# Laying out softmax denominators by DMA instead of TensorE in a fused attention and FFN block

## The chip, the cores and the metric

One core of one Trainium2 chip runs the kernel. The metric is the device time of one execution in microseconds (us); lower is better. A core has five engines with instruction streams of their own (TensorE or PE, VectorE or DVE, ScalarE or ACT, GpSimd or POOL, SyncE or SP) and DMA engines that the SP queue feeds here.

## The reference

Four batches of 1024 tokens with 128 features go through a layer norm, then grouped-query attention (16 heads of width 64, K and V projected to 512 columns and repeated twice) and a small FFN of hidden size 384; both results are added to the input. All is float32.

```python
xq = rope(q @ Wq); xk = jnp.repeat(rope(kv @ Wk), 2, axis=-1)
xv = jnp.repeat(kv @ Wv, 2, axis=-1)
scores = softmax(xq @ xk * scale, axis=-1)
out = (scores @ xv) @ Wo
h = silu(x @ wg.T) * (x @ wu.T);  ffn = h @ wd.T
x = x + attention(layernorm(x)) + ffn(layernorm(x))
```

The repeat makes neighbouring columns of K and V equal, so the kernel works with 32 distinct features per head (`E` = 32).

## The kernel before

A prologue (about the first 107 us) does the layer norm, the whole FFN and the first projections. After it come 16 steps (4 batches by 4 groups `g` of 4 heads) of two units each; unit `u` = 2s + t is one half of the queries (512 columns, `HALF`) of step `s`. Each of the 32 units has one slot of the main loop. All five streams are written out by hand; they meet only by semaphores, each engine takes its instructions in order, and all DMAs of the loop go through SP's queue.

In slot `u` TensorE (lines 532 to 651) makes, interleaved over eight key tiles `kt`: the scores of unit `u` (line 542, ACT turns each into `prob`, line 799); 16 score tiles of unit `u+1` for its row maxima (`max_tile`, line 379, two places in PSUM; DVE reduces each, line 853, and PE needs the place of tile m-2 free before tile m); the product with V (line 394); the denominators of unit `u-1` (lines 404 and 407); the output projection of unit `u-2` (line 430); and the projections for unit `u+4` (lines 361 and 369).

The part that is changed brings the output of unit `u-1` to `o_norm`. The denominators stand in `bank_m` as 128 x 512: each of four heads has its 512 numbers repeated on 32 partitions. ACT copies them to `den` (`read_den`, line 766, at kt 2). PE transposes `den` in four blocks at kt 3 (`transpose_den`, line 414), so that a head's 512 numbers lie on 128 partitions; DVE inverts the 128 x 16 that are distinct (line 950, after maxima tile 9); ACT spreads them (line 771, at kt 4); PE transposes back (`transpose_inv`, line 421, at kt 5); and DVE multiplies (`normalise`, line 956). `normalise` stands in DVE's order after the 16th tile and `split_max` (lines 859 and 861), and ahead of `pair_sum` (line 946) and `rotate` (lines 844 to 848). `rotate` frees the PSUM places of the projections; the first two maxima tiles of the next slot wait for its two `rope_done` signals (line 560).

SP's order in step `s` (lines 293 to 333), of which the first part falls into slot 2s: an x load (four steps have one: 0, 2, 6 and 10), 12 packs of the lower half (`pack_heads(1 - n, 0)`, 128 KB each), weights, tables (2 MB), V, `wo_stage`, 12 packs of the upper half, V, and the maxima of unit 2s+1 (`pack_max`). The second part falls into slot 2s+1: once a batch the store of the output and a reload of `y_acc`, then the maxima of unit 2s+2. Slot 2s+1 starts on PE only once all 26 packs of step `s` have landed (line 576).

## Time and profile before

| | us |
|---|---|
| runs (3): median, lowest, highest | 1169.87, 1164.29, 1173.73 |
| the profiled execution | 1166.32 |
| its span, first to last instruction | 1164.4 |
| busy: PE, DVE, POOL, ACT | 1118.8, 886.7, 877.2, 733.7 |
| mean granted clock of TensorE | 0.989 |
| one slot of the main loop | 32.6 |

A line of the lists below has the source line, the engine, the operation, what is written and read, how often, the busy time and the mean in ns of one, and the idle time of the engine ahead of it with what ended it. A timeline's line starts with the start time and the duration in us. SPq is the queue of SyncE; its lines show how long it took to issue DMAs, not the transfers. Times in the text without a slot named are those of slot 14 (step 7), which runs from about 567 to 599.5 us, or of slot 15 behind it.

### The profile page before, as it was taken

What the parts mean: (1) busy time and instruction counts of PE and PEld (TensorE: products, weight loads), DVE (VectorE), ACT (ScalarE), POOL (GpSimd) and SP (SyncE); (2) the same over time, 40 slices, a digit from 0 to 9 for tenths busy, and PEclk for the clock granted to TensorE, in tenths of its full rate; (3) what the DMA queues carried; (4) which work ended last, traced back from release to release, by engine and by line L of the source; (5) the groups of instructions that cost most, each with busy time, mean ns of one, the idle gap of its engine ahead of it and who ended that gap; (6) DMA issues with size and microseconds to landing.
All of it is one profiled execution on the core that took longest, in us unless ns stands there. A gap on an engine that the chain in (4) does not pass through costs nothing.

```text
span 1164.4 us, 17083 instructions
## 1 busy us (share of the span) xinstructions
PE 1118.8 (96%) x6288; PEld 661.8 (57%) x6288; DVE 886.7 (76%) x1009; ACT 733.7 (63%) x1330; POOL 877.2 (75%) x274
## 2 busy tenths in 40 slices
PE   5899999999999999999999999999999999999986
PEld 4787555555555565555555555555556555554432
DVE  7686777778787887778787887778788787777721
ACT  3333666666676666766666666666666666666663
POOL 3222778887778888877778887878778887888776
PEclk9899999999999999999999999999999999999999
DMA  6662808071441618071441618071431617050000
GB/s 230 167 258 87 238 2 224 1 222 40 111 115 35 191 37 224 2 222 40 115 110 39 187 37 224 1 218 44 122 105 45 181 37 225 1 130 2 4 1 18
DMA packets 56305, 124.97 MB, mean 107 GB/s; under 512 B 7968, under 2 KB 19488, under 8 KB 54048
## 3 DMA queue, kind: packets, MB, share of 16 engines
q1 hardware_dynamic: 56224, 123.89, 36.8%
q8 instruction: 50, 0.82, 0.3%
q14 instruction: 31, 0.25, 0.1%
HBM read 53.08 MB, written 10.49 MB: 55 GB/s over the span
## 4 chain that ended last, share of the span: by engine, by line
PE 80%; DVE 15%; ACT 2%; issue 1%; POOL 1%; DMA 1%; POOLq 0%; ACTq 0%; DVEq 0%
PE bank_o L394 20%; PE bank_s L542 19%; PE scores L379 18%; DVE row_max L853 13%; PE scores L361 7%; PE bank_m L369 3%; PE bank_m L430 2%; PE bank_m L407 2%; PE bank_m L404 2%; ACT prob L799 2%; PE scores L480 2%; PE bank_s L497 1%; POOL prob_sum L1048 1%; PE bank_o L497 1%; PE bank_m L497 1%
## 5 line engine op out<-in xcount | busy, mean ns | idle before, releaser
L799 ACT ACTIVATE prob<-bank_s 128x512 f32<-128x512 f32 x1024 | 595.5, 600 | 253.4 <-PE bank_s L542 230.0
L853 DVE TENSOR_REDUCE row_max<-scores 128x1 f32<-128x1024 f32 x512 | 597.0, 1214 | 201.3 <-PE scores L379 201.1
L1048 POOL TENSOR_TENSOR prob_sum<-prob_sum,prob 128x2048 f32<-128x2048 f32 x96 | 439.3, 4576 | 13.9 <-ACT prob L799 0.5
L542 PE MATMUL bank_s<-qk_pack 98*128 98x512 f32 x1024 | 431.0, 437 | 8.2 <-ACT prob L799 5.9
L379 PE MATMUL scores<-qk_pack 96*128 96x512 f32 x1024 | 337.4, 411 | 9.0 <-DVE row_max L853 1.4
L542 PEld LDWEIGHTS bank_s<-qk_pack 98*128 98x128 f32 x1024 | 192.9, 189 | 195.1 <-issue 86.9
L394 PE MATMUL bank_o<-prob,v 128*32 128x512 f32 x2048 | 250.0, 606 | 0.0
L1048 POOL TENSOR_TENSOR prob_sum<-prob_sum,prob_pair 128x2048 f32<-128x2048 f32 x32 | 147.2, 4601 | 104.3 <-DVE prob_pair L946 104.3
L379 PEld LDWEIGHTS scores<-qk_pack 96*128 96x128 f32 x1024 | 180.1, 190 | 73.8 <-DVE row_max L853 52.3
L992 POOL TENSOR_TENSOR qk_stage<-rope,qk_stage 128x512 fp32r<-128x512 f32 x64 | 82.0, 1283 | 91.1 <-ACT qk_stage L685 91.1
L1040 POOL TENSOR_TENSOR prob_sum<-prob 128x2048 f32<-128x2048 f32 x32 | 146.8, 4587 | 0.0
L394 PEld LDWEIGHTS bank_o<-prob,v 128*32 128x32 f32 x2048 | 53.8, 110 | 121.5 <-issue 72.7
L361 PE MATMUL scores<-x_stage,w_stage 128*128 128x512 f32 x336 | 98.7, 402 | 0.0
L766 ACT COPY den<-bank_m 128x512 f32<-128x512 f32 x32 | 18.8, 587 | 91.8 <-PE bank_m L407 91.8
L946 DVE TENSOR_TENSOR prob_pair<-prob 128x2048 f32<-128x2048 f32 x32 | 73.8, 2306 | 1.4 <-ACT prob L799 1.4
L361 PEld LDWEIGHTS scores<-x_stage,w_stage 128*128 128x128 f32 x336 | 61.5, 190 | 14.8
L369 PEld LDWEIGHTS bank_m<-w_stage,x_stage 128*128 128x128 f32 x336 | 46.3, 191 | 3.6
L1056 POOL TENSOR_TENSOR y_acc<-y_part,y_acc 128x512 f32<-128x512 f32 x32 | 40.9, 1279 | 8.9 <-ACT y_part L777 8.9
L844 DVE TENSOR_TENSOR scores<-scores,table 128x512 f32<-128x512 f32 x64 | 44.2, 691 | 2.5 <-PE scores L361 2.5
L848 DVE TENSOR_TENSOR rope<-scores,rope 128x512 f32<-128x512 f32 x64 | 44.3, 692 | 2.2
L369 PE MATMUL bank_m<-w_stage,x_stage 128*128 128x128 f32 x336 | 43.8, 266 | 0.0
L846 DVE TENSOR_TENSOR rope<-scores,table 128x512 f32<-128x512 f32 x64 | 43.5, 679 | 0.1
(88 smaller groups left out, 685.0 us busy)
## 6 DMA issues: line engine op xcount, KB each, us to landing
qk_pack<-qk_stage SPq DMA_DIRECT2D x384, 128.0 KB, 4.7
table<-tables SPq DMA_DIRECT2D x16, 2048.0 KB, 9.7
w_stage<-w_scratch SPq DMA_DIRECT2D x14, 640.0 KB, 4.5
v<-v_stage SPq DMA_DIRECT2D x32, 256.0 KB, 7.9
xT_scratch<-xT_hl SPq DMA_DIRECT2D x4, 1024.0 KB, 10.1
x_stage<-xT_scratch SPq DMA_DIRECT2D x4, 1024.0 KB, 6.5
w_scratch<-w_split SPq DMA_DIRECT2D x1, 2560.0 KB, 15.5
x_all<-x SPq DMA_DIRECT2D x4, 512.0 KB, 11.7
```

The costliest lines, as they stand in the source:

```text
L361: last = mm(scores[:, c, :], w_from[:, a, c, :], x_from[:, r, cols], start=n == 0, stop=n == 2)
L369: last = mm(bank_m[:, j * 128:(j + 1) * 128], x_from[:, r, at:at + 128], w_from[:, a, 4, :], start=n == 0, stop=n == 2)
L379: last = mm(scores[:, 2 * (m % places) + c, :], qk_pack[n][0:SPLIT_K, 0, t, h, (m % QT) * 128:(m % QT + 1) * 128], qk_pack[n][0:SPLIT_K, 1 ...
L394: last = mm(bank_o[h * E:(h + 1) * E, :], v_sb[n][:, kt, h * E:(h + 1) * E], prob[:, kt % RING, h, :], start=kt == 0, stop=kt == KT - 1)
L542: mm(bank_s[:, h % 2, :], qk_pack[j][0:SCORE_K, 1, kt // QT, h, (kt % QT) * 128:(kt % QT + 1) * 128], qk_pack[j][0:SCORE_K, 0, t, h, :], s ...
L799: A(prob[:, kt % RING, h, :], bank_s[:, h % 2, :], ACT.Exp).then_inc(prob_ready, 1)
L848: V.tensor_tensor(rope[:, 2 * k, :], scores[:, 2 * k, :], rope[:, 2 * k + 1, :], ALU.add).then_inc(rope_done, 1)
L853: V.tensor_reduce(row_max[:, m:m + 1], scores[:, at:at + 2, :].rearrange("p c k -> p (c k)"), axis=AX.X, op=ALU.max).then_inc(max_read, 1)
L946: V.tensor_tensor(prob_pair[:], prob[:, 4 % RING], prob[:, 5 % RING], ALU.add).then_inc(pair_done, 1)
L992: TT(qk_stage[:, 2 * k + 1, t, :], rope[:, 2 * k, :], qk_stage[:, 2 * k, t, :].bitcast(F32), ALU.subtract).then_inc(lo_done, 1)
L1040: TT(prob_sum[:, t], prob[:, 0], prob[:, 1], ALU.add).then_inc(sum_done, 1)
L1048: TT(prob_sum[:, t], prob_sum[:, t], part, ALU.add).then_inc(sum_done, 1)
```

## The change

- The denominators: SP issues `lay_den`, a DMA that takes one partition of each head from `den` (4 x 512) and lays it out as 64 x 32 in `den_rows`. DVE inverts these 64 x 32 (after maxima tile 11, before it was 9), `save_inv` stores them in DRAM (8 KB), and `spread_inv` reads them back into `den`, each head's row on 32 partitions (256 KB written). Each of the three waits for the one before. `normalise` then reads `den` in place of `bank_m`.
- Both groups of four transposes on PE, the spreading copy on ACT and the small inverse from PSUM are gone from each unit.
- In an even slot the three DMAs of unit 2s-1 are put among the upper packs: `lay_den` before them, `save_inv` after six of the twelve, `spread_inv` after nine. In an odd slot those of unit 2s come after `pack_max` (and after the store and reload, where there is one) and before the next `pack_max`.
- `load_tables` and its wait move ahead of the lower packs.
- PE's transpose of the maxima waits for `den_read` instead of `o_done`; `read_den` waits for the `o_done` of the unit before.
- The last unit has no DMA: DVE inverts all 128 x 512 of `bank_m` into `den`.

```diff
--- before.py
+++ after.py
@@ -69,7 +69,7 @@
 NE = HG
-INVERT_AFTER = 9
+INVERT_AFTER = 11
 def build(nc, x, tables, w_qkv, wo_even, wo_odd, w_gu, w_down, ident_in, out):
@@ -81,6 +81,7 @@
     xT_dram = nc.dram_tensor("xT_scratch", (128, 2, B * S), F32, kind="Internal").ap()
     w_dram = nc.dram_tensor("w_scratch", (128, G, 2, NW), F32, kind="Internal").ap()
     y_dram = nc.dram_tensor("y_scratch", (128, NT, D), F32, kind="Internal").ap()
+    inv_dram = nc.dram_tensor("inv_scratch", (HG, HALF), F32, kind="Internal").ap()
     ctx = ExitStack()
     with ctx:
@@ -107,7 +108,8 @@
         max_rows = keep("max_rows", [2 * TILES, 128])
         o_raw = keep("o_raw", [128, HALF])
         den = keep("den", [128, HALF])
-        den_inv = keep("den_inv", [128, QT, HG])
+        den_rows = keep("den_rows", [2 * E, HALF // QT // 4])
+        inv_rows = keep("inv_rows", [2 * E, HALF // QT // 4])
         y_part = keep("y_part", [128, HALF])
         o_norm = keep("o_norm", [128, HALF])
         y_acc = keep("y_acc", [128, KT, D])
@@ -176,8 +178,8 @@
         score_ready, prob_ready, pv_done, pair_done, sum_done, den_ready = (sem("score_ready"),
             sem("prob_ready"), sem("pv_done"), sem("pair_done"), sem("sum_done"), sem("den_ready"))
-        o_read, den_read, denT_ready, inv_done, inv_spread, inv_ready = (sem("o_read"), sem("den_read"),
-            sem("denT_ready"), sem("inv_done"), sem("inv_spread"), sem("inv_ready"))
+        o_read, den_read, den_laid, inv_done, inv_saved, inv_spread = (sem("o_read"), sem("den_read"),
+            sem("den_laid"), sem("inv_done"), sem("inv_saved"), sem("inv_spread"))
         o_done, y_ready, y_read, y_added = sem("o_done"), sem("y_ready"), sem("y_read"), sem("y_added")
         block = ctx.enter_context(nc.Block())
@@ -233,8 +235,8 @@
                     sp.dma_start(qk_pack[n][r * E:(r + 1) * E, :, t, h, :].bitcast(F32),
                                  qk_stage[h * E:(h + 1) * E, parts, t, :].bitcast(F32)).then_inc(done, 16)
-            def pack_heads(n, t):
-                for h in range(HG):
+            def pack_heads(n, t, heads=range(HG)):
+                for h in heads:
                     pack_head(n, t, h, packed)
             def pack_v(n, t):
@@ -287,6 +289,21 @@
             for n in range(4):
                 sp.wait_ge(y_saved[n], 16 * len(range(n, CHUNKS, 4)) - (16 if n < 2 else 0))
+            def lay_den(u):
+
+                sp.wait_ge(den_read, u + 1)
+                sp.dma_start(den_rows[:], den[0:128:E, :]).then_inc(den_laid, 16)
+
+            def save_inv(u):
+
+                sp.wait_ge(inv_done, u + 1)
+                sp.dma_start(inv_dram.rearrange("h (r c) -> (h r) c", c=HALF // QT // 4), inv_rows[:]).then_inc(inv_saved, 16)
+
+            def spread_inv(u):
+
+                sp.wait_ge(inv_saved, 16 * u + 16)
+                sp.dma_start(den[:], inv_dram.unsqueeze(1).to_broadcast([HG, E, HALF])).then_inc(inv_spread, 16)
+
             def store_out(b):
                 sp.dma_start(out[bass.ds(b, 1)].rearrange("b (n p) d -> p (b n) d", p=128), y_acc[:]).then_inc(out_done, 16)
@@ -299,6 +316,8 @@
                     sp.wait_ge(proj_ready, 10 * s + 20)
                     if new_x:
                         load_x(b + 1 if nxt % G == 0 else b)
+                    sp.wait_ge(rope_done, 4 * s + 8)
+                    load_tables(nxt % G)
                 if not (last_pair and n == 1):
                     at_least(sp, score_ready, 64 * s)
@@ -308,17 +327,25 @@
                     if new_x:
                         sp.wait_ge(xb_in, 16 * (b + (2 if nxt % G == 0 else 1)))
                     load_w(nxt % G)
-
-                    sp.wait_ge(rope_done, 4 * s + 8)
-                    load_tables(nxt % G)
                 if not (last_pair and n == 1):
                     sp.wait_ge(v_staged, 2 * s + 3)
                     at_least(sp, pv_done, 16 * s)
                     pack_v(1 - n, 0)
                 sp.dma_start(wo_stage[n][:], wo_sum[:, g, :]).then_inc(wo_in, 16)
-                if not (last_pair and n == 1):
+                more = not (last_pair and n == 1)
+                if s > 0:
+                    lay_den(2 * s - 1)
+                if more:
                     sp.wait_ge(lo_done, 4 * s + 8)
-                    pack_heads(1 - n, 1)
+                    pack_heads(1 - n, 1, range(2))
+                if s > 0:
+                    save_inv(2 * s - 1)
+                if more:
+                    pack_heads(1 - n, 1, range(2, 3))
+                if s > 0:
+                    spread_inv(2 * s - 1)
+                if more:
+                    pack_heads(1 - n, 1, range(3, HG))
                     sp.wait_ge(v_staged, 2 * s + 4)
                     pack_v(1 - n, 1)
                 pack_max(2 * s + 1, n, 1)
@@ -329,6 +356,9 @@
                     store_out(b - 1)
                     sp.wait_ge(out_done, 16 * b)
                     sp.dma_start(y_acc[:], y_dram[:, bass.ds(b * KT, KT), :]).then_inc(y_in, 16)
+                lay_den(2 * s)
+                save_inv(2 * s)
+                spread_inv(2 * s)
                 if not (last_pair and n == 1):
                     pack_max(2 * s + 2, 1 - n, 0)
@@ -406,20 +436,6 @@
                 for h in range(HG):
                     last = mm(bank_m[h * E:(h + 1) * E, :], ones[:], prob_sum[:, t, h, :], start=False, stop=True)
                 last.then_inc(den_ready, 1)
-
-            def transpose_den(u):
-
-                pe.wait_ge(den_read, u + 1)
-                for j in range(QT):
-                    last = nc.tensor.transpose(bank_m[:, j * 128:(j + 1) * 128], den[:, j * 128:(j + 1) * 128], ident[:])
-                last.then_inc(denT_ready, 1)
-
-            def transpose_inv(u):
-
-                pe.wait_ge(inv_spread, u + 1)
-                for j in range(QT):
-                    last = nc.tensor.transpose(bank_m[:, j * 128:(j + 1) * 128], den[:, j * 128:(j + 1) * 128], ident[:])
-                last.then_inc(inv_ready, 1)
             def project_out(u, n, s):
@@ -604,8 +620,6 @@
                         score(kt, 3)
                         maxima()
                     elif kt == 3:
-                        if not is_first(u):
-                            transpose_den(u - 1)
                         score(kt, 1)
                         maxima()
                         score(kt, 2)
@@ -620,8 +634,6 @@
                         score(kt, 3)
                         maxima()
                     elif kt == 5:
-                        if not is_first(u):
-                            transpose_inv(u - 1)
                         score(kt, 1)
                         maxima()
                         score(kt, 2)
@@ -634,7 +646,7 @@
                         score(kt, 2)
                         if do_max:
-                            at_least(pe, o_done, u)
+                            at_least(pe, den_read, u)
                             transpose_max(v)
                         project_chunk(1)
                         score(kt, 3)
@@ -660,8 +672,6 @@
             pv(UNITS - 1, KT - 1, 1)
             project_out(UNITS - 2, 1, STEPS - 1)
             denominators(UNITS - 1, 1)
-            transpose_den(UNITS - 1)
-            transpose_inv(UNITS - 1)
             project_out(UNITS - 1, 1, STEPS - 1)
@@ -762,14 +772,8 @@
             def read_den(u):
                 act.wait_ge(den_ready, u + 1)
-                at_least(act, inv_ready, u)
+                at_least(act, o_done, u)
                 nc.scalar.copy(den[:], bank_m[:]).then_inc(den_read, 1)
-
-            def spread_inv(u):
-
-                act.wait_ge(inv_done, u + 1)
-                nc.scalar.copy(den[:].rearrange("p (j h e) -> p j h e", j=QT, h=HG),
-                               den_inv[:].unsqueeze(3).to_broadcast([128, QT, HG, E])).then_inc(inv_spread, 1)
             def read_y(u):
                 act.wait_ge(y_ready, u + 1)
@@ -810,8 +814,6 @@
                                 round_hi(1, u + 3, 1 - t, s + 1 + t)
                             if not first:
                                 read_den(u - 1)
-                        elif (kt, h) == (4, 1) and not first:
-                            spread_inv(u - 1)
                         elif (kt, h) == (6, 2) and not (last_pair and j == 1 and t == 1):
                             read_maxT(u + 1)
@@ -826,8 +828,6 @@
             pairs_of_steps(body)
             read_o(UNITS - 1)
             read_y(UNITS - 2)
-            read_den(UNITS - 1)
-            spread_inv(UNITS - 1)
             read_y(UNITS - 1)
@@ -946,14 +946,24 @@
                 V.tensor_tensor(prob_pair[:], prob[:, 4 % RING], prob[:, 5 % RING], ALU.add).then_inc(pair_done, 1)
             def invert(u):
-                dve.wait_ge(denT_ready, u + 1)
-                V.reciprocal(den_inv[:], bank_m[:].rearrange("p (j h e) -> p j h e", j=QT, h=HG)[:, :, :, 0]).then_inc(inv_done, 1)
+                dve.wait_ge(den_laid, 16 * u + 16)
+                at_least(dve, inv_saved, 16 * u)
+                V.reciprocal(inv_rows[:], den_rows[:]).then_inc(inv_done, 1)
             def normalise(u):
-                dve.wait_ge(inv_ready, u + 1)
+                dve.wait_ge(inv_spread, 16 * u + 16)
                 dve.wait_ge(o_read, u + 1)
                 at_least(dve, y_ready, u)
-                V.tensor_tensor(o_norm[:], o_raw[:], bank_m[:], ALU.mult).then_inc(o_done, 1)
+                V.tensor_tensor(o_norm[:], o_raw[:], den[:], ALU.mult).then_inc(o_done, 1)
+
+            def normalise_last(u):
+                dve.wait_ge(den_ready, u + 1)
+                dve.wait_ge(o_done, u)
+                V.reciprocal(den[:], bank_m[:]).then_inc(inv_done, 1)
+                dve.wait_ge(inv_done, u + 1)
+                dve.wait_ge(o_read, u + 1)
+                dve.wait_ge(y_ready, u)
+                V.tensor_tensor(o_norm[:], o_raw[:], den[:], ALU.mult).then_inc(o_done, 1)
             def slot(i, j, t, last_pair):
                 u = 4 * i + 2 * j + t
@@ -978,8 +988,7 @@
                         slot(i, j, t, last_pair)
             pairs_of_steps(body)
-            invert(UNITS - 1)
-            normalise(UNITS - 1)
+            normalise_last(UNITS - 1)
         @block.gpsimd
```

## Rows read from the trace of the kernel before

**Rows 1.** The page: busy times, and the chain that ended last, by engine.

```profile
PE 1118.8 (96%) x6288; PEld 661.8 (57%) x6288; DVE 886.7 (76%) x1009; ACT 733.7 (63%) x1330; POOL 877.2 (75%) x274
...
PE 80%; DVE 15%; ACT 2%; issue 1%; POOL 1%; DMA 1%; POOLq 0%; ACTq 0%; DVEq 0%
```

**Rows 2.** Groups of instructions by line: the first of the two groups of transposes.

```profile
L414 PE MATMUL bank_m<-ident,den 128*128 128x128 f32 x128 | 19.3, 272 | 0.7 <-ACT den L766 0.7
```

**Rows 3.** Chain of waits in slot 14: start, us on the chain, what.

```profile
580.93 2.37 DVE row_max L853 x2
583.34 0.74 PE scores L379 x2
...
588.30 2.37 DVE row_max L853 x2
590.71 0.74 PE scores L379 x2
```

**Rows 4.** Timeline of TensorE, slot 14 and the start of slot 15.

```profile
581.66 0.60 PE L414 MATMUL bank_m<-ident,den 128*128 128x128 f32 x4
582.02 0.48 PE L542 MATMUL bank_s<-qk_pack 98*128 98x512 f32 x1
...
589.03 0.60 PE L421 MATMUL bank_m<-ident,den 128*128 128x128 f32 x4
...
600.88 0.62 PE L379 MATMUL scores<-qk_pack 96*128 96x512 f32 x2
```

**Rows 5.** Timeline of VectorE, slot 14 and the start of slot 15.

```profile
584.50 2.29 DVE L853 TENSOR_REDUCE row_max<-scores 128x1 f32<-128x1024 f32 x2
588.30 4.62 DVE L853 TENSOR_REDUCE row_max<-scores 128x1 f32<-128x1024 f32 x4 [1.52 <-PE scores L379]
...
593.85 0.18 DVE L861 TENSOR_TENSOR max_hl<-row_max,max_hl 128x16 f32<-128x16 f32 x1
...
600.00 0.69 DVE L848 TENSOR_TENSOR rope<-scores,rope 128x512 f32<-128x512 f32 x1
```

**Rows 6.** Timeline of ScalarE in slot 14: the denominators' copy.

```profile
580.07 0.59 ACT L766 COPY den<-bank_m 128x512 f32<-128x512 f32 x1 [2.85 <-PE bank_m L407]
```

**Rows 7.** Timeline of the SP queue in slot 14: the packs' issue.

```profile
567.25 8.89 SPq L233 DMA_DIRECT2D qk_pack<-qk_stage  x12
...
578.66 10.82 SPq L233 DMA_DIRECT2D qk_pack<-qk_stage  x12
```

**Rows 8.** GB/s from 582 to 598 us, 40 slices of 0.4 us.

```profile
GB/s 369 451 451 246 451 82 246 287 149 343 344 391 288 211 256 277 251 215 256 302 236 236 292 266 215 236 246 266 200 67 31 0 0 0 0 0 0 0 36 5
```

**Rows 9.** DMA issues: count, KB each, median us from issue to landing.

```profile
out<-y_acc SPq DMA_DIRECT2D x4, 512.0 KB, 2.9
y_acc<-y_scratch SPq DMA_DIRECT2D x3, 512.0 KB, 3.8
...
y_scratch<-y_part SPq DMA_DIRECT2D x1, 256.0 KB, 2.0
```

**Rows 10.** 595.8 to 599.8 us, slices of 0.1 us: DMA busy tenths, GB/s.

```profile
DMA  0000000000000011110000000000000000000000
GB/s 0 0 0 0 0 0 0 0 0 0 0 0 0 0 31 26 41 46 21 0 0 0 0 0 0 0 0 0 0 0 0 0 0 0 0 0 0 0 0 0
```

**Rows 11.** 419 to 424 us, slices of 0.125 us: the reload of y_acc.

```profile
GB/s 86 0 0 0 0 0 0 0 0 0 0 131 131 131 197 229 131 131 262 229 131 197 328 393 393 426 230 197 164 131 33 0 0 0 0 0 0 0 0 0
```

**Rows 12.** 416 to 420 us, slices of 0.1 us: the store of y_acc.

```profile
GB/s 0 0 0 0 0 0 0 0 0 0 0 0 0 0 36 256 353 348 333 358 353 348 333 358 353 348 333 358 353 313 103 5 0 0 0 0 0 0 0 0
```

**Rows 13.** Groups by line and shape: the reciprocals of the prologue.

```profile
L875 DVE RECIPROCAL rstd<-rstd 128x24 f32<-128x24 f32 x1 | 0.3, 303 | 0.3 <-ACT rstd L700 0.3
L875 DVE RECIPROCAL rstd<-rstd 128x8 f32<-128x8 f32 x1 | 0.2, 202 | 0.3 <-ACT rstd L700 0.3
```

**Rows 14.** Timeline of the kernel's end: the last unit's denominators.

```profile
1154.21 0.59 ACT L766 COPY den<-bank_m 128x512 f32<-128x512 f32 x1 [2.52 <-PE bank_m L407]
...
1157.20 0.69 DVE L956 TENSOR_TENSOR o_norm<-o_raw,bank_m 128x512 f32<-128x512 f32 x1 [1.40 <-PE bank_m L421]
```


## The prediction, made before the changed kernel was run

> **What bounds the kernel now.** I read the page first: TensorE is busy for 1118.8 of 1164.4 us, and the chain that ended last is 80% PE but 15% DVE [rows 1]. So PE work is worth its time only where the chain runs over PE. The groups by line give the size of what is removed: two groups of transposes, 19.3 us over the whole run for the first [rows 2] and as much for the second, 38.6 us together, or 1.2 us in each of 32 slots. The chain of one slot then tells where they lie. Twice in a slot it leaves PE for two maxima reductions on DVE, from 580.93 to 583.34 and from 588.30 to 590.71, and comes back to PE at a maxima tile [rows 3]. PE's timeline puts the first transposes at 581.66 and the second at 589.03 [rows 4]: both inside the stretches in which PE's next maxima tile waits for a place that DVE has yet to read. Neither line 414 nor 421 is in the chain. From 590.71 to the next slot PE sets the pace, and DVE follows it closely: `rotate` of slot 14 ends at 600.00 + 0.69 = 600.69 [rows 5], and PE's second maxima tile of slot 15, which waits for it, starts at 600.88 [rows 4]. That is 0.19 us of slack for everything on DVE between `split_max` and there, `normalise` first.
>
> **The transposes go.** 38.6 us of PE work is hidden by the two DVE stretches. Tiles 10 and 15 start at 583.34 and 590.71 because DVE then gives their place back; with the transposes gone PE reaches them earlier and waits. I take 0. If that cover weren't there, PE would advance by what the next matmul starts later for each group; bounds are 0 and 38.6 us, and at most 19.3 us if one of the two groups counts.
>
> **The copy and the inverse.** The spreading copy on ACT is worth nothing: ACT is busy for 733.7 us and waits for PE [rows 1]. The inverse moves behind tile 11. DVE's tiles 10 and 11 take 584.50 to 586.79 and tile 12 starts at 588.30, after 1.52 us of idle time [rows 5]. The new inverse has 32 elements a partition; two old ones took 202 ns for 8 and 303 for 24 [rows 13], 6.3 ns for each more, so 32 take 0.35 us. It is free if `den_rows` has landed by 588.30 - 0.35 = 587.95; if not, DVE holds tile 12 and, behind it, the whole second stretch and PE, one for one.
>
> **When `den_rows` lands, even slots.** `den` is written at 580.07 + 0.59 = 580.66 [rows 6]. In steps 1 to 13 the tables now go first, at about 568.0 (when `rope_done` comes). Ahead of `lay_den` lie 2.10 MB of tables, 12 x 0.131 of packs, 0.66 of weights, 0.26 of V and 0.07 of `wo_stage`: 4.65 MB. In before's busy stretch the tables came at some 430 GB/s and the packs at 250 [rows 8]. 2.10 MB / 430 + 2.55 MB / 250 = 4.9 + 10.2 = 15.1 us from about 569.3, the time of the first packets: 584.4. SP has its issues out by then: 12 packs at 8.89/12 = 0.74 to 10.82/12 = 0.90 us each [rows 7] and three more give 579 to 581. With some 0.5 to 1 us for the last packets `den_rows` is there at about 585.2, and at 587 in the three steps with an x load (1 MB more, begun a microsecond earlier). Both are before 587.95, so I take no wait; the reserve is 1 to 2.7 us.
>
> **Save and spread.** The inverse ends at 586.79 + 0.35 = 587.14. A store to DRAM on an idle queue took 2.0 us from issue to landing [rows 9]; I take 2.1 for these 8 KB, in an even slot up to 3.5 behind six packs. Meanwhile SP issues the three packs that stand before `spread_inv`: after a save issue of 0.6 us, three at 0.74 to 0.90, so `spread_inv` is issued at 590.0 to 590.7. How long it takes the trace doesn't show: it writes 256 KB from four rows. First packets come 1.3 us after issue: 597.2 against a `pack_max` issue that followed 595.93 [rows 10]. Then there are three rates. At full width, as the store of `y_acc` at 350 GB/s [rows 12], 256 KB take 0.75 us, and with 0.5 us to land 2.55 us in all. At the rate of a transfer with few partitions: `pack_max` writes 2 partitions, keeps about one tenth of the DMA engines busy and moves 46 GB/s at its best [rows 10]; twice as many rows give 92 GB/s, 2.85 us, 4.65 in all. At the rate of a read from scratch DRAM: `y_acc` took from 420.4 to 422.8 for 512 KB, 218 GB/s over all engines [rows 11]; a quarter of that is 55 GB/s, 4.8 us, 6.6 in all. I take 4.65, since the source has four rows and the nearest row with few rows behaves so.
>
> The Trainium skill (DMA: Bandwidth & Descriptors, section "Rules for kernel authors") says that an outermost dimension below 16, a leading zero-stride broadcast for one, confines a DMA to at most that many engines. By that rule `spread_inv` has four engines and not sixteen, so it speaks against this change; the tenth of the engines in [rows 10] agrees, with two partitions. By a sixteen-engine transfer the sum below would be 0 instead of 14 us.
>
> **The even slots.** Landing at 590.0 + 4.65 to 590.7 + 4.65 plus up to 0.3 for the packs ahead: 594.7 to 595.7. `normalise` could start at 593.85 + 0.18 = 594.03 [rows 5] and has 0.19 us of slack: 594.22. It waits 0.5 to 1.5 us beyond that, 1.0 in the middle. Behind it on DVE stand `pair_sum` and `rotate`, and PE's maxima tile 1 waits for `rotate`, so this is paid in full. Fourteen even slots have packs (steps 1 to 14): 7 to 21, middle 14 us. The upper packs and V end some 3 us later than before, at about 598, still before PE asks for them near 599.7.
>
> **The odd slots.** SP is idle there, `lay_den` lands long before tile 11. The inverse ends one slot later at 619.8, save 621.9, spread 626.6. `normalise` can start at 594.03 + 32.65 = 626.7. No wait, by a hair. In the three slots with a store and reload `lay_den` waits for 2.9 + 3.8 us of these [rows 9], and is just in time.
>
> **The tail.** The last denominators are ready at 1154.21 and `normalise` starts at 1157.20, 2.99 us later [rows 14]. The new inverse of 512 elements takes 0.20 + 504 x 0.0063 = 3.4 us: +0.4 us.
>
> **The sum.** 1166.32 + 0 + 14 + 0.4 = 1180.7 us for an execution like the profiled one. That one lies 3.55 us below the median of 1169.87, so 1184 us.
>
> **Rivals.**
> - *All three transfers are hidden (0.29).* `spread_inv` goes at full width, lands at 593.3 at the latest, and nothing is left but the tail: 1170 us. For it: 0.9 us of reserve, and the sum's wait hangs on one rate. Against: [rows 10].
> - *Both kinds of slot wait (0.15).* At 55 GB/s the spread takes 6.6 us: even slots wait 3.0 us x 14 = 42, odd ones 621.9 + 6.6 - 626.9 = 1.6 us x 16 = 26. That is 1169.9 + 68 = 1238 us; half of it, 1204, at a rate between. For it: the slow read in [rows 11].
> - *`den_rows` lands late (0.10).* The queue ahead of it is slower than 250 GB/s, or `pack_heads` is issued more slowly behind the tables. At 588.95, 1 us beyond the point where it decides, 13 slots pay 1 us each and the save and spread shift as well: 1170 + 13 + 14 = 1197 us.
> - *The transposes did cost PE time (0.08).* The other side: PE's next score starts 0.36 us after the start of the first group, 582.02 against 581.66 [rows 4], and the second is its like: 0.72 us x 31 slots = 22 us. 1148 us if every transfer is hidden too. It decides if PE, not DVE, releases tiles 10 and 15. Against: the chain, which has DVE there in slot after slot.
>
> **How the numbers follow.** The forecast, a wait in the even slots alone, has 0.38, with its own range 1177 to 1192. With the rivals' 0.29, 0.15, 0.10 and 0.08 that is 1. About 1% is what a measurement of this kernel can tell from no change: 11.7 us. Faster by more: 0.08. Within: all of the hidden case, the forecast where each even slot waits less than 0.8 us (some 0.14 of its 0.38), a little of the others: 0.45. Slower: 0.47. The range goes from 1166, below the hidden case, to 1220, which leaves out the faster case and the slow end of the second rival.
>
> **What would show it.** In the changed profile the PE waits for the maxima reductions should grow by about the transposes' time with tiles 10 and 15 unmoved against the slot's start. The wait of `o_norm` for the DMA into `den` should be about 1 us in 14 slots and near 0 in the others; the even slots should be longer by as much. `den_rows` should be there before tile 11 is reduced. The landing of `spread_inv` from its issue is the number on which most hangs: 2.6 and I am wrong towards no change, 6.6 and it is much slower. A slot shorter than 32.6 us would refute the zero for the transposes.

## The result and the profile after

The changed kernel takes 1254.29 us (median of 4 runs, 1242.84 to 1260.61), the kernel before 1171.62: a ratio of 1.0713, interval 1.0661 to 1.0765. It is 7% slower, where 1184 was forecast and the range ended at 1220. The profiled execution has a span of 1251.9 us, 87.5 more than before's 1164.4 (the medians are 82.7 apart), and a mean granted clock of 0.951 where before had 0.989. Of the runs further below, one execution with the tables back (3563 us) and one with the added wait of 3.35 us (1744 us) were in a slow state and are left out of their medians and ratios.

The page of the changed kernel: busy times, and the chain that ended last by engine and by line.

```profile
PE 1160.2 (93%) x6032; PEld 640.7 (51%) x6032; DVE 895.3 (72%) x1009; ACT 710.4 (57%) x1297; POOL 874.8 (70%) x274
...
PE 52%; DVE 17%; DMA 15%; SPq 10%; issue 3%; ACT 1%; POOL 1%; POOLq 0%; DVEq 0%; ACTq 0%
PE bank_o L424 14%; PE scores L409 12%; PE bank_s L558 11%; DVE row_max L853 9%; SPq L235 8%; DMA den<-inv_scratch 6%; DMA den_rows<-den 5%; PE scores L391 4%; DVE prob_pair L946 3%; DMA inv_scratch<-inv_rows 3%; DVE rope L848 2%; PE bank_m L437 2%; PE bank_m L434 2%; PE bank_m L446 2%; PE scores L496 2%
```

Against [rows 1], PE has 256 matmuls fewer and 41 us more of busy time, and a quarter of the chain is now DMA and the SP queue: the spread (line 305), the layout (line 295), the save, and the packs between them. The waits, in total, times and the longest:

```profile
DVE o_norm L957 <- DMA den<-inv_scratch: 57.8, 18, 6.7
...
PEld scores L409 <- DVE rope L848: 43.3, 30, 2.8
DVE inv_rows L951 <- DMA den_rows<-den: 32.8, 11, 18.1
```

Neither DMA wait existed before. The longest of each (6.7 and 18.1) belongs to the last slot, where DVE has nothing else to do. The second line is how they reach PE: the next slot's maxima tiles wait for `rotate`, which stands behind `normalise`.

ScalarE's copy of the denominators comes at the same place of each slot and is paced by PE, so the distance from one to the next is the length of a slot. Its timeline, slots 12 to 15:

```profile
549.58 0.59 ACT L776 COPY den<-bank_m 128x512 f32<-128x512 f32 x1 [2.85 <-PE bank_m L437]
...
588.60 0.58 ACT L776 COPY den<-bank_m 128x512 f32<-128x512 f32 x1 [2.85 <-PE bank_m L437]
...
621.22 0.58 ACT L776 COPY den<-bank_m 128x512 f32<-128x512 f32 x1 [2.85 <-PE bank_m L437]
...
659.77 0.59 ACT L776 COPY den<-bank_m 128x512 f32<-128x512 f32 x1 [2.85 <-PE bank_m L437]
```

From an even slot's copy to the odd one's it takes 39.02 and 38.55 us, from an odd one's to the even one's 32.62, level with the 32.65 of before. So nearly all of the loss lies between an even slot's middle and the next. Over the run, 13 such intervals of the even slots 2 to 26 add 81.6 us to 13 x 32.65, 14 odd ones add 0.7, the last three intervals 3.1, start and tail together 2.5. Before's own intervals hold 0.4 more than 32.65 each, which leaves 87.5. DVE's timeline shows the two waits that an even interval can hold, and that the odd one between has none (549 to 639 us):

```profile
558.53 0.34 DVE L951 RECIPROCAL inv_rows<-den_rows 64x32 f32<-64x32 f32 x1 [2.33 <-DMA den_rows<-den]
...
568.16 0.69 DVE L957 TENSOR_TENSOR o_norm<-o_raw,den 128x512 f32<-128x512 f32 x1 [4.41 <-DMA den<-inv_scratch]
...
595.14 0.33 DVE L951 RECIPROCAL inv_rows<-den_rows 64x32 f32<-64x32 f32 x1
...
602.49 0.69 DVE L957 TENSOR_TENSOR o_norm<-o_raw,den 128x512 f32<-128x512 f32 x1
...
628.05 0.34 DVE L951 RECIPROCAL inv_rows<-den_rows 64x32 f32<-64x32 f32 x1 [0.21 <-DMA den_rows<-den]
...
638.27 0.69 DVE L957 TENSOR_TENSOR o_norm<-o_raw,den 128x512 f32<-128x512 f32 x1 [3.09 <-DMA den<-inv_scratch]
```

In the 13 even intervals the waits of `o_norm` sum to 47.5 us (2.1 to 4.9 each) and those for `den_rows` to 14.7 us (0 to 5.6). These may not simply be added: what each is worth is read where the clock stays up, in the kernel with four spreads further below. At a clock of 1.00 its even intervals with a wait of `o_norm` take 32.65 us plus that wait plus 0.05, to within 0.01 us, as long as the wait for `den_rows` is at most 2.1 us; at 2.38 and 2.53 us of it they take 0.26 and 0.41 more. So the first 2.1 us of a wait for `den_rows` cost nothing by themselves, though they do make the spread later. By that rule the changed kernel pays 47.5 us for `o_norm`, 13 x 0.05 = 0.7 for slack that is gone, and 3.8 directly for `den_rows` (3.5 of it in slot 4, which waited 5.58). The remaining 29.6 us, 2.3 an interval (1.7 to 3.0), go with the lower clock. Whole intervals from copy to copy, slot 12 of the changed kernel and slot 12 of the one with four spreads; the third number from the end is the granted clock:

```profile
549.58:588.60 39.02, 36.16 (x178) 18.21 (x179) 25.72 (x27) 21.18 (x40) 26.55 (x9) 0.91 0.43 105
520.99:555.32 34.33, 32.64 (x178) 17.86 (x179) 25.73 (x27) 21.17 (x39) 26.62 (x9) 1.00 0.47 119
```

The first had waits of 2.33 and 4.41 us and lies 1.7 above the rule, the second of 2.12 and 1.64 and fits it. All 13 even intervals of the changed kernel have a mean clock of 0.88 to 0.95. In five of them PE also waited up to 1.1 us for the packs of the maxima or of V; these lie no further above the rule (1.9 to 2.4 us) than the other eight (1.7 to 3.0), so that wait isn't a second cost that can be told apart. Busy times by stretch behind the wait that ended at 568.16:

```profile
572.00:576.00 4.00, 2.27 (x11) 1.11 (x14) 3.93 (x7) 1.67 (x4) 3.86 (x2) 0.99 0.00 0
576.00:580.00 4.00, 4.00 (x19) 0.98 (x16) 1.16 (x2) 1.10 (x3) 4.00 (x1) 0.58 0.00 0
```

PE idles for 1.7 us between 572 and 576, waiting for `rotate`, and then works from 576 to 580 at a mean of 0.58, mostly at the lower level of 1.2 GHz.

### The profile page after: what moved, and what is told of

Read it like the earlier page. It is cut to its first block, busy times and chain, and to the rows that moved or that the text cites. A ratio compares the mean times of both kernels' runs of the same rounds, so it can differ in the third digit from the quotient of the medians.

```text
span 1251.9 us, 16671 instructions
## 1 busy us (share of the span) xinstructions
PE 1160.2 (93%) x6032; PEld 640.7 (51%) x6032; DVE 895.3 (72%) x1009; ACT 710.4 (57%) x1297; POOL 874.8 (70%) x274
## 4 chain that ended last, share of the span: by engine, by line
PE 52%; DVE 17%; DMA 15%; SPq 10%; issue 3%; ACT 1%; POOL 1%; POOLq 0%; DVEq 0%; ACTq 0%
PE bank_o L424 14%; PE scores L409 12%; PE bank_s L558 11%; DVE row_max L853 9%; SPq L235 8%; DMA den<-inv_scratch 6%; DMA den_rows<-den 5%; PE scores L391 4%; DVE prob_pair L946 3%; DMA inv_scratch<-inv_rows 3%; DVE rope L848 2%; PE bank_m L437 2%; PE bank_m L434 2%; PE bank_m L446 2%; PE scores L496 2%
## 5 line engine op out<-in xcount | busy, mean ns | idle before, releaser
L803 ACT ACTIVATE prob<-bank_s 128x512 f32<-128x512 f32 x1024 | 588.8, 599 | 360.1 <-PE bank_s L558 340.2
L558 PE MATMUL bank_s<-qk_pack 98*128 98x512 f32 x1024 | 435.6, 441 | 14.1 <-ACT prob L803 7.7
L409 PE MATMUL scores<-qk_pack 96*128 96x512 f32 x1024 | 354.1, 428 | 46.7 <-DVE rope L848 30.8
L424 PE MATMUL bank_o<-prob,v 128*32 128x512 f32 x2048 | 273.7, 656 | 0.0
L424 PEld LDWEIGHTS bank_o<-prob,v 128*32 128x32 f32 x2048 | 56.6, 115 | 135.4 <-issue 82.3
L776 ACT COPY den<-bank_m 128x512 f32<-128x512 f32 x31 | 18.2, 586 | 87.6 <-PE bank_m L437 87.6
L957 DVE TENSOR_TENSOR o_norm<-o_raw,den 128x512 f32<-128x512 f32 x31 | 23.4, 755 | 58.0 <-DMA den<-inv_scratch 57.8
```

Of the source, the lines that this page charges most:

```text
L409: last = mm(scores[:, 2 * (m % places) + c, :], qk_pack[n][0:SPLIT_K, 0, t, h, (m % QT) * 128:(m % QT + 1) * 128], qk_pack[n][0:SPLIT_K, 1 ...
L424: last = mm(bank_o[h * E:(h + 1) * E, :], v_sb[n][:, kt, h * E:(h + 1) * E], prob[:, kt % RING, h, :], start=kt == 0, stop=kt == KT - 1)
L558: mm(bank_s[:, h % 2, :], qk_pack[j][0:SCORE_K, 1, kt // QT, h, (kt % QT) * 128:(kt % QT + 1) * 128], qk_pack[j][0:SCORE_K, 0, t, h, :], s ...
L803: A(prob[:, kt % RING, h, :], bank_s[:, h % 2, :], ACT.Exp).then_inc(prob_ready, 1)
```

## The experiments

**Was the removed work worth anything?** The kernel before without transposes, inverse and spreading copy, and with no DMA in their place:

```diff
-                            transpose_den(u - 1)
...
-                            transpose_inv(u - 1)
...
-                            spread_inv(u - 1)
...
-                            invert(u - 1)
...
-                V.tensor_tensor(o_norm[:], o_raw[:], bank_m[:], ALU.mult)
+                V.tensor_tensor(o_norm[:], o_raw[:], den[:], ALU.mult)
```

(It multiplies by the denominators themselves; the waits on the removed parts go to `den_read` and `o_done`.)

> The kernel before without both groups of transposes, the inverse and the spreading copy; it multiplies by the denominators instead of dividing by them, so it leaves the inverse out, and has no DMA in their place. It shows what the removed work was worth by itself. Theory (the transposes lie in the two stretches in which DVE's maxima set the pace): within 0.5% of the kernel before, 1166 to 1177 us. Rival (PE is 96% busy, so its work counts): 1135 to 1150 us.

Measured: 1173.4 us, ratio to before 1.0039 (1.0011 to 1.0067). ScalarE's timeline of this kernel:

```profile
547.28 0.59 ACT L760 COPY den<-bank_m 128x512 f32<-128x512 f32 x1 [2.85 <-PE bank_m L407]
...
579.90 0.58 ACT L760 COPY den<-bank_m 128x512 f32<-128x512 f32 x1 [2.85 <-PE bank_m L407]
```

A slot takes 32.62 us without 1.2 us of PE work in it; before it took 32.65. PE's timeline has idle time where the chain of [rows 3] had put DVE, ahead of tiles 10 and 15:

```profile
583.18 0.73 PE L379 MATMUL scores<-qk_pack 96*128 96x512 f32 x2 [0.16 <-DVE row_max L844]
...
590.54 0.74 PE L379 MATMUL scores<-qk_pack 96*128 96x512 f32 x2 [0.17 <-DVE row_max L844]
```

These two tiles start 3.28 and 10.64 us after ScalarE's copy, where before they started 3.27 and 10.64 after it (580.07, 583.34 and 590.71): they didn't move, so in the slots of the main loop the removed work was hidden whole. In the last slots, which have no projections, four intervals take 33.62, 33.88, 31.90 and 28.16 us against 30.71, 30.71, 31.11 and 24.18 before, 10.9 us more; behind the last copy, where nothing covers the transposes, it takes 2.4 us less. The spans are 1172.3 and 1164.4, the mean clocks 0.976 and 0.989. That the removed work was worth something in those last slots isn't shown: of the 19 executions of the kernel before that the last kernels below are compared with, ten took 1171.8 to 1176.4 us at a clock of 0.979 to 0.983, like this one, and the profiled one (1166.32 us) is like the other nine.

**What does a wait of DVE cost by itself?** The kernel before with a DVE reciprocal on a tile of its own ahead of `normalise` in 15 even slots, no DMA added; once of 512 elements (3.35 us), once of 130 (0.96 us):

```diff
+                if t == 0 and not is_first(u):
+                    dve.wait_ge(pad_done, u // 2)
+                    V.reciprocal(pad[:, 0:512], pad[:, 0:512]).then_inc(pad_done, 1)
                 if not is_first(u):
                     normalise(u - 1)
```

> The kernel before with one added DVE instruction of about 3.4 us, a reciprocal on a tile of its own, ahead of normalise in the 15 even slots from slot 2 on; nothing else is changed and no DMA is added. It has the wait of the changed kernel without its cause. Theory (a wait of PE is followed by a stretch at the lower clock): 15 x (3.4 - 0.2) = 48 us for the wait itself plus 1.5 to 2 us each for the clock, 1240 to 1250 us, with a granted clock of 0.95 to 0.97. Rival (a wait costs its own length only): 1218 to 1222 us and a clock of 0.985 or more.

> The kernel before with an added DVE reciprocal of 130 elements, about 1.0 us, ahead of normalise in 15 even slots, where the earlier one took 3.4 us. Theory of the forecast (a wait is paid at its own length less the slack): 15 x 0.8 = 12 us, 1182 us. Rival (each wait brings the lower clock, as with 3.4 us): 1195 us or more. A third way (short waits are absorbed): within 4 us of the kernel before.

Measured: 1231.02 us with 3.35 us (ratio 1.0507, 1.0447 to 1.0567), 1184.33 with 0.96 us (1.0109, 1.0075 to 1.0143). With 3.35 us the 13 even intervals fall into two groups: five take 35.8 us, 3.2 more than 32.65, and eight take 37.0 to 37.25, 4.3 to 4.6 more. The first group pays the wait less the slack; the second pays 1.2 to 1.4 us on top. One of the eight and one of the five from copy to copy; the third number from the end is the clock:

```profile
465.80:502.94 37.14, 34.06 (x186) 19.92 (x187) 29.55 (x28) 22.02 (x40) 26.68 (x9) 0.95 0.38 114
535.55:571.36 35.81, 32.76 (x186) 18.84 (x187) 29.46 (x28) 22.01 (x40) 26.67 (x9) 1.00 0.38 124
```

And the idle time of PE in each of the two, from its timeline:

```profile
483.64 0.40 PE L388 MATMUL bank_m<-ident,max_hl 128*32 128x128 f32 x1 [2.79 <-DVE o_norm L959]
...
553.39 0.28 PE L388 MATMUL bank_m<-ident,max_hl 128*32 128x128 f32 x1 [2.77 <-DVE o_norm L959]
```

PE idles for 2.8 us in one piece in both; behind the first the clock falls (0.63 from 484 to 488 us), behind the second it stays at 1.00. What decides between them these runs don't show. The mean clock is 0.967. In the profiled execution with 0.96 us, the quickest of its ten, every even interval takes 33.40 to 33.46, 0.78 more, and the clock is 0.992. So the forecast's way of pricing a short wait (length less 0.19 us) was right here, but a wait of 3.35 us also brings the clock down in most slots. I had expected it in each; that is why 1240 to 1250 was too much. The changed kernel fits: its intervals have a clock of 0.91 and cost 2.3 us on top, these eight 0.95 and 1.3. PE's idle time isn't in the same place, though: here it waits for `o_norm` to transpose the maxima, there for `rotate`.

**Is the spread slow because it has four rows?** Four DMAs, one a head, in place of one:

```diff
-                sp.dma_start(den[:], inv_dram.unsqueeze(1).to_broadcast([HG, E, HALF])).then_inc(inv_spread, 16)
+                for h in range(HG):
+                    sp.dma_start(den[h * E:(h + 1) * E, :], inv_dram[h:h + 1, :].to_broadcast([E, HALF])).then_inc(inv_spread, 16)
```

(`normalise` then waits for 64 a unit and not 16.)

> The changed kernel with the spread of the inverse as four DMAs, one for each head, each from one row to 32 partitions. Theory (the one DMA with four source rows runs on a quarter of the DMA engines and takes 2.4 us longer than need be): despite three more issues of 0.6 us on SP, the spread is there sooner; the wait of o_norm in even slots falls from 3 to 4.6 us to 1 to 3 us, and the kernel takes 1205 to 1235 us. Rival (the spread is slow because it queues behind the packs, whatever its width): the three more issues come on top, the wait grows by 1 to 2 us in each even slot, 1265 to 1290 us.

Measured: 1192.07 us, ratio 1.0196 (1.0129 to 1.0263): 62 us less than the changed kernel, with the same bytes and three more issues. The waits of `o_norm` fall from 57.8 to

```profile
DVE o_norm L958 <- DMA den<-inv_scratch: 15.1, 10, 5.1
```

of which 5.1 is the last slot's; those for `den_rows` stay at 32.2 us, 18.4 of it in the last slot (32.8 and 18.1 in the changed kernel). In the 13 even slots of the changed kernel the spread took 6.3 to 7.0 us from its issue to `o_norm`, on an otherwise idle queue, where it made `o_norm` wait, 4.9 to 5.4. The four take 3.3 to 4.2 us in the even slots in which `o_norm` waited, and 3.3 in the last one. So other traffic adds some 1.5 us to the one DMA and little to the four. The transfers themselves are seen best in an odd slot, where nothing else moves. DMA busy tenths and GB/s of the changed kernel, 597 to 603 us in slices of 0.15 us; the one DMA was issued at 597.22:

```profile
DMA  0000000000112125212222222222111100000000
GB/s 0 0 0 0 0 0 0 0 0 0 41 55 82 68 96 96 82 55 82 82 96 96 109 109 109 82 96 96 55 55 55 41 14 0 0 0 0 0 0 0
```

And of the kernel with four, 563.5 to 569.5 us, issued from 563.96 on:

```profile
DMA  1000000001442542545572000000000000000000
GB/s 18 0 0 0 0 0 0 0 0 55 178 178 96 178 164 96 178 137 109 82 178 96 27 0 0 0 0 0 0 0 0 0 0 0 0 0 0 0 0 0
```

The DMA issues of the same kernel: count, KB each, us to landing:

```profile
den<-inv_scratch SPq DMA_DIRECT2D x124, 64.0 KB, 2.0
```

One DMA keeps one to two tenths of the engines busy for 23 slices, 3.4 us; four keep them busy for 14 slices, 2.1 us, at four tenths in the mean, and even so they are issued only every 0.43 us. The Trainium skill (DMA: Bandwidth & Descriptors, "Rules for kernel authors") says that an outermost dimension below 16 confines a DMA to at most that many engines. Here it is the four heads, and the 2 tenths of the first trace agree with it. The difference of 62 us is what the one DMA costs here, the clock behind its waits included.

**Is it SP's queue that makes `den_rows` late?** The layout issued from ScalarE right behind its copy and no longer from SP, once with the four spreads and once with the single one:

```diff
                 nc.scalar.copy(den[:], bank_m[:]).then_inc(den_read, 1)
+                act.wait_ge(den_read, u + 1)
+                nc.scalar.dma_start(den_rows[:], den[0:128:E, :]).then_inc(den_laid, 16)
```

> The kernel with four spreads, and the layout of the denominators issued from ACT right behind its copy instead of from SP. Theory (den_rows is late in even slots because its DMA stands in SP's queue behind tables and packs): it lands within 2 to 4 us of its issue, DVE no longer waits for it, and the kernel takes 1172 to 1182 us, level with the kernel that leaves the inverse out (1173 us). Rival (the DMA engines are simply full then, whichever queue is used): den_rows stays late, 1187 to 1195 us.

> The changed kernel with only the layout of the denominators issued from ACT; the spread is the one DMA again. Theory (two separate costs): the waits for den_rows go, those of o_norm for the spread stay at 3 to 4 us in 14 even slots and bring the lower clock with them: 1225 to 1240 us. Rival (the late den_rows is what makes the spread late): the o_norm waits shrink below 1.5 us and it takes 1195 us or less.

Measured: 1193.95 us with four spreads (ratio 1.0203, 1.0147 to 1.0258), level with 1192.07 from SP; 1262.14 with one (1.0768, 1.0711 to 1.0826), no better than the changed kernel. The theory fell. The changed kernel's trace speaks against it too: SP issued the layout within 0.4 us of the end of ScalarE's copy in ten of the 13 even slots (in slot 14 at 622.06, the copy ended at 621.80) and 1.3 to 1.6 us behind it in the three with an x load. The timeline of the first kernel, ScalarE's queue and then DVE:

```profile
595.27 0.54 ACTq L771 DMA_DIRECT2D den_rows<-den  x1
...
603.21 0.34 DVE L946 RECIPROCAL inv_rows<-den_rows 64x32 f32<-64x32 f32 x1 [1.71 <-DMA den_rows<-den]
```

These 8 KB take 7.9 us on a queue that holds nothing else. In the last slot of the changed kernel, with no traffic, the same DMA was issued at 1215.88 and DVE started at 1217.66, 1.8 us later. The second kernel had neither wait mended (62.0 us for `o_norm`, 29.8 for `den_rows`), so it separates nothing. That they are two costs is shown by the kernel with four spreads, where one shrank and the other stayed.

**Is it what the DMA engines have to move?** The kernel with four spreads, but each table load brings 16 of 128 partitions, 256 KB and not 2 MB (the rotation then has wrong tables on the others):

```diff
-                sp.dma_start(table[:].rearrange("p t c q -> p (t c q)"),
-                             tables[bass.ds(g, 1)].rearrange("g p t c q -> p (g t c q)")).then_inc(table_in, 16)
+                sp.dma_start(table[0:16].rearrange("p t c q -> p (t c q)"),
+                             tables[bass.ds(g, 1), 0:16].rearrange("g p t c q -> p (g t c q)")).then_inc(table_in, 16)
```

> The kernel with four spreads, and the table load of each step cut to 16 of 128 partitions, 256 KB in place of 2 MB (the rotation then uses the first group's tables on the other partitions). Theory (den_rows is late because the DMA engines themselves are full of tables, packs and weights at that time; another queue didn't help): with 1.8 MB less ahead of it den_rows is in time in every slot, the waits for it and most of those for the spread are gone, 1172 to 1180 us. Rival (the layout with its small pieces is slow beside any packs): the waits stay, 1186 to 1194 us.

Measured: 1176.34 us, ratio 1.0060 (1.0027 to 1.0092). The waits:

```profile
DVE inv_rows L952 <- DMA den_rows<-den: 18.5, 2, 18.3
DVE o_norm L958 <- DMA den<-inv_scratch: 5.3, 2, 5.0
```

Outside the last slot 0.2 and 0.3 us are left, and the intervals of the main loop take 32.6 us (one 33.0). What is left against before lies mostly in the last slots (33.49, 33.82 and 32.03 us, as in the kernel without an inverse) and behind them. How busy the DMA engines are while the layout of slot 14 waits in the changed kernel, 622 to 630 us in slices of 0.2 us:

```profile
DMA  9999999999798899899999999999999999999675
```

So `den_rows` is late because the DMA engines still have tables, packs and weights to move; the queue that it is issued from makes no difference. Not tested is whether the layout, which reads four rows as well, would land sooner in another shape.

**Does the place of the tables matter?** The changed kernel with the load put back behind the weights:

```diff
                     load_w(nxt % G)
+                    sp.wait_ge(rope_done, 4 * s + 8)
+                    load_tables(nxt % G)
```

(The two lines are gone from their place ahead of the packs.)

> The changed kernel with one edit undone: the tables are loaded after the weights again, behind the lower packs. Theory (the loss is latency of the three chained DMAs on the one queue, and the clock that falls behind each wait): the queue ahead of the denominators' layout holds the same bytes either way, so den_rows still lands late in many even slots and the spread still lands about 6.5 us after its issue; within 1.5% of the changed kernel's 1254 us, that is 1235 to 1273. Rival (the tables' move is what hurts): close to 1190 us or below.

Measured: 1253.33 us, ratio 1.0714 (1.0654 to 1.0774), the changed kernel's time. Waits of `o_norm` 58.5 us, for `den_rows` 27.5 (18.2 in the last slot). Moving the tables ahead neither helps nor hurts, as it should be if the same bytes are under way when the denominators come.

**Can the cover be taken away, so that the transposes count?** Two attempts to spread the maxima tiles better over PE's order in the kernel before. In the first, tiles 7 and 12 move between the halves of the product with V:

```diff
+                def pv_spaced(kt):
+                    pv(u, kt - 2, j)
+                    maxima()
+                    pv(u, kt - 1, j)
...
-                        pv_pair(kt)
+                        pv_spaced(kt)
```

> The kernel before, transposes and all, with two maxima tiles of each slot moved ahead on PE: tile 7 and tile 12 each between the two halves of the product with V. Theory (twice a slot DVE's reductions set the pace because four tiles come to PE at once): the two stretches shrink and a slot takes 31.0 to 31.6 us, 1125 to 1145 us in all. Rival (the order of the tiles doesn't matter, PE's work does): 1160 to 1175 us.

> The kernel that leaves out transposes, inverse and spreading copy, with the same two tiles moved. Theory (once DVE no longer covers them, the transposes are on the path): 0.4 to 0.9 us a slot below the kernel before with the tiles moved, 12 to 28 us less than that one. Rival (they are still covered, or the granted clock falls in the gaps): no more than 5 us less, or slower than it.

Measured: 1193.57 us (1.0192, 1.0151 to 1.0234) with the transposes and 1193.0 (1.0184, 1.0143 to 1.0224) without them. Slots are 33.5 us in both, and not 31.0 to 31.6. The chain of the first, around the denominators:

```profile
522.72 0.90 PE bank_m L407 x8
...
523.64 0.58 ACT den L769
524.23 0.51 ACT prob L802
...
524.78 0.50 PE bank_s L542
```

The tile that used to stand behind the denominators was what PE did while ScalarE copied them; with it gone PE waits 1.1 us for the copy and the exponential behind it. The second attempt (code not shown) keeps it, splits only the product at key tile 2, and drops the last tile of key tile 5:

> The kernel before with maxima tiles moved another way: one more tile between the two halves of the product with V at key tile 2, all those after it stay where they were on PE but one place earlier in number, and the last one of key tile 5 falls away; so no score is left without a tile beside it after the denominators. Theory (the first attempt left ScalarE's copy and exponentials alone on the path after the denominators; tiles spread over PE's long groups shorten DVE's stretches): a slot of 31.7 to 32.3 us, 1140 to 1160 us. Rival (splitting the product with V costs what the spacing gains): 1166 to 1180 us.

> The same order of tiles in the kernel that leaves out transposes, inverse and spreading copy. Theory (the transposes are worth something only when DVE's stretches no longer cover them): 8 to 22 us less than the kernel before with this order. Rival (still covered): within 4 us of it.

Measured: 1190.84 us (1.0181, 1.0120 to 1.0242) and 1184.47 (1.0134, 1.0076 to 1.0191), slots of 33.34 and 33.26 us, and not 31.7 to 32.3. The chain of the first has one DVE stretch left in place of two, but the pieces with a tile between them are longer:

```profile
517.18 0.99 PE bank_o L394 x8
518.18 0.66 PE scores L379 x2
518.84 0.99 PE bank_o L394 x8
```

2.64 us, where the product in one piece and a tile take 1.85 + 0.47 in the same chain. That is 0.3 of the 0.7 us that a slot got longer; where the rest comes from was not found. The transposes are worth 0.08 us a slot of the main loop there, so they are still covered; the medians are 6.4 us apart and the profiled spans 3.6, between the two forecasts of 4 and of 8 to 22. These four runs point to no version better than before.

## Why the prediction was wrong

**The transposes at 0: right.** Leaving them out changed a slot by 0.03 us, and tiles 10 and 15 stayed where they were. The rival in which they cost PE time was refuted, and with it the whole gain of the change.

**The inverse at 0.35 us: right. The tail at 0.4: right for its term, short for the whole.** The inverse took 0.33 to 0.35. The last unit's, of 512 elements, was put at 3.4 us:

```profile
1240.03 3.36 DVE L962 RECIPROCAL den<-bank_m 128x512 f32<-128x512 f32 x1 [10.46 <-PE bank_m L437]
```

From the last denominators to `normalise` it takes 3.40 us where it took 2.99. Behind ScalarE's copy in the last slot the kernel takes 2.3 us more in all, 0.9 of it in the last output projection, which took 2.08 us against 1.16 at a granted clock of 0.56 (0.95 before).

**Odd slots without a wait: right, by the hair that was forecast.** 14 odd intervals add 0.7 us together.

**`den_rows` in time: wrong.** The step said that 4.65 MB would be moved by 584.4 and `den_rows` would be there at 585.2, with a reserve of 1 to 2.7 us. SP's queue had it issued as forecast:

```profile
622.06 0.62 SPq L295 DMA_DIRECT2D den_rows<-den  x1
...
628.42 0.50 SPq L300 DMA_DIRECT2D inv_scratch<-inv_rows  x1
...
631.87 0.57 SPq L305 DMA_DIRECT2D den<-inv_scratch  x1
```

From 622.06 to its landing it took 6.0 us, not 4; in the other slots that waited for it 6.1 to 7.3, and up to 10.4 with an x load. The wait put at 0 measured 14.7 us over 13 slots. What failed is that everything ahead would be moved by 584.4. This was the rival with 0.10. The part of such a wait that is free was too small in the forecast, too: 587.95 - 586.79 = 1.2 us, where the four-spread kernel shows 2.1, so that only 3.8 us were paid directly. A late `den_rows` also makes save and spread later.

**The spread at 4.65 us: the right mechanism, mis-sized.** I took the rate of `pack_max`, scaled to four rows, 92 GB/s. On an idle queue the packets ran for 3.4 us at 77 GB/s (0.262 MB / 3.4), and where an odd slot waited it was 4.9 to 5.4 us from issue to `o_norm`. In the 13 even slots it was 6.3 to 7.0 (631.87 to 638.27 is 6.4), 6.6 in the mean, where at most 0.3 us had been added for the packs ahead. At 4.65 us each the 13 waits would have been 25.1 us shorter. The middle wait of 1.0 us measured 3.65, and 14 us became 47.5; the 22.4 that the spread's length doesn't account for hold the 13 that were forecast and some 9 for a spread issued later, behind a late `den_rows` and a save after which the spread was issued 2.5 to 5.1 us later. The rival at 55 GB/s had even slots nearly right (3.0 us) and odd ones wrong (1.6): the slow part is not the read from DRAM alone, which the four DMAs do as well, but a DMA on few engines beside the packs.

**The upper packs in time: not in every slot.** They were to end at about 598, before PE asks for them. In five even intervals PE waited up to 1.1 us for packs of the maxima or of V.

**The clock at nothing: missing.** The sum treated a wait as its own length. 29.6 us of the 87.5 come on top of the waits in the 13 even intervals. With four spreads twelve of the 13 intervals kept a clock of 1.00 and had nothing on top. The added waits show the same with no DMA in play: nothing at 0.96 us, 1.2 to 1.4 us in eight of 13 at 3.35.

Put together: 47.5 + 0.7 + 3.8 + 29.6 = 81.6 in the even intervals, 0.7 in the odd ones, 3.1 in the last slots and 2.5 at start and tail, less the 0.4 that before's intervals hold over 32.65, is 87.5 us. The forecast was 14.4.

## What to carry to other kernels

Before work is taken off the busiest engine, look where it lies in the chain of waits: 38.6 us of PE work here stood, but for the last unit's, under another engine's stretch, and its removal bought nothing in the main loop. A chain of small DMAs is priced by what is in flight when each is issued, which a duration on an idle queue doesn't show, and by how many rows its outermost dimension has. Waits can't be added up before each has been checked for what it delays: 14.7 us of one kind cost 3.8 directly. And a wait behind which the clock falls costs more than its length, 2.3 us more here.

## What the runs showed of the hardware

- 8 KB from SBUF to SBUF in 64 pieces: 1.8 us from issue to use on idle DMA engines (last slot), 6.0 to 7.3 beside full ones and up to 10.4 with an x load ahead, and not sooner from ScalarE's own queue (7.9 us) than from SP's.
- 256 KB read from four DRAM rows: one DMA 3.4 us of packets at one to two tenths of the engines, 4.9 to 5.4 us from issue to use when idle and 6.3 to 7.0 beside other traffic; four DMAs of 64 KB landed 2.0 us after issue each, all four 3.3 us after the first issue when idle and 3.3 to 4.2 beside other traffic.
- 8 KB stored to DRAM and read back: the spread was issued 1.7 us after the save (595.50 and 597.22), in an even slot 2.5 to 5.1 (272.65 and 275.12, 413.26 and 418.36).
- DVE's reciprocal: 6.3 ns for each element of a partition from 8 to 512 elements (202 ns and 3.36 us).
- The same PE idle time of 2.8 us in a busy stretch was followed by a lower granted clock in eight of 13 intervals and not in five; where it was, the interval took 1.2 to 1.4 us more.
